# A graph kernel's attention and second spline: join and scans at the block's end, copies by the vector engine

## The reference

```python
# layer 0, attention with 4 heads: per edge a score, softmax over a node's edges, weighted sum
e = leaky_relu(a_src[:, src] + a_dst[:, dst] + fc_b[0], 0.2)
seg_max = segment_max(e.T, src)
e = exp(e - seg_max.T[:, src])
att = e / segment_sum(e.T, src).T[:, src]
agg = segment_sum(att * hp[:, dst, :], src)
...
# layer 3, second spline convolution: 125 kernels of 64 x 64, 8 of them weighted by a basis per edge
basis, idx = spline_basis(pseudo)
msg = einsum('es,eso->eo', basis, (x @ W)[col * K + idx])
out = segment_sum(msg, row) / max(deg, 1) + b
```

## Time and profile before

| what | us |
|---|---|
| median of 3 runs | 7320.52 (7303.47 to 7342.39) |
| the profiled execution | 7357.94 |
| its span | 7355.8 |
| PE busy | 4635.6 (63%) |
| DVE busy | 4183.0 (57%) |
| ACT busy | 1654.2 (22%) |
| POOL busy | 4443.2 (60%) |

### The profile page before, as it was taken

The page is one execution under the profiler, slowest core; times in us unless marked ns, Lnnn a source line. Parts: engine busy times, 40 slices in busy tenths (PEclk is TensorE's granted clock), DMA queues, the critical chain, the costliest instruction groups (busy, mean ns, idle before and its releaser), DMA issues. The chain is left out here.

```text
span 7355.8 us, 95916 instructions
## 1 busy us (share of the span) xinstructions
PE 4635.6 (63%) x31067; PEld 3408.4 (46%) x31067; DVE 4183.0 (57%) x9381; ACT 1654.2 (22%) x2811; POOL 4443.2 (60%) x4319
## 2 busy tenths in 40 slices
PE   5444442876638888888554667999992444544433
PEld 4444442655536666665443434555552333333322
DVE  7555553769946666666442316777773445444433
ACT  1111120117824444444231000000000222222211
POOL 2777776000057777777433256777764777777763
PEclk9999999569979999999776788999996777777766
DMA  4222221013332222224866581111111111111385
GB/s 73 78 71 78 71 78 26 21 36 151 160 76 54 52 53 53 54 52 49 37 30 180 195 270 39 38 37 37 37 34 23 19 18 18 19 19 18 17 14 14
DMA packets 388448, 441.47 MB, mean 60 GB/s; under 512 B 241139, under 2 KB 312320, under 8 KB 387981
## 3 DMA queue, kind: packets, MB, share of 16 engines
q0 software_dynamic: 137696, 130.26, 18.3%
q1 hardware_dynamic: 191113, 286.63, 12.4%
q10 hardware_dynamic: 59568, 23.69, 1.4%
HBM read 358.46 MB, written 82.34 MB: 60 GB/s over the span
## 5 line engine op out<-in xcount | busy, mean ns | idle before, releaser
L951 POOL DMA_INDIRECT at_far<-att_table,at_rec x1184 | 1227.7, 1037 | 886.0 <-DMA at_rec<-rec_r 400.9
L1524 POOL DMA_INDIRECT p_far<-table,p_rec x1184 | 1242.1, 1049 | 488.2 <-issue 359.9
L2162 PE MATMUL g_l_ps_sum<-g_l_row,g_l_of 128*128 128x392 f32 x3224 | 1062.9, 493 | 19.4 <-DVE g_l_of L2113 19.4
L534 POOL DMA_INDIRECT rec_r<-so_r_rec,so_r_place x806 | 835.0, 1036 | 245.5 <-issue 245.5
L2084 POOL DMA_INDIRECT g_l_got<-table,g_l_index x806 | 811.1, 1006 | 245.5 <-issue 228.4
L2162 PEld LDWEIGHTS g_l_ps_sum<-g_l_row,g_l_of 128*128 128x128 f32 x3224 | 613.2, 190 | 469.7 <-DVE g_l_of L2113 20.6
L1422 PE MATMUL p_ps_outer<-p_spread,p_basis 128*25 128x40 f32 (+1 forms) x4736 | 758.9, 341 | 77.9 <-DVE p_spread L1367 53.1
L1422 PEld LDWEIGHTS p_ps_outer<-p_spread,p_basis 128*25 128x25 f32 (+1 forms) x4736 | 636.0, 183 | 207.6 <-issue 94.5
L1422 PE MATMUL at_bank<-p_spread,p_basis 64*125 64x256 f32 x4736 | 629.3, 418 | 107.1 <-ACT p_outer L1477 107.1
L2096 DVE TENSOR_SCALAR g_l_row<-g_l_iota,edge_row 128x784 f32<-128x784 f32 x806 | 500.3, 693 | 222.2 <-PE g_l_ps_sum L2162 222.0
L489 PE MATMUL so_r_look<-so_r_table,so_r_lo_t 128*128 128x26 f32 x1612 | 425.0, 433 | 310.8 <-DVE so_r_table L433 310.8
(11 more groups left out here) (457 smaller groups left out, 6201.2 us busy)
## 6 DMA issues: line engine op xcount, KB each, us to landing
adjacent<-ad_by_chunk SPq DMA_DIRECT2D x74, 800.0 KB, 3.3
so_r_row<-pad_src SPq DMA_DIRECT2D x62, 832.0 KB, 6.2
g_l_counts<-adjacent SPq DMA_DIRECT2D x60, 800.0 KB, 6.9
g_l1d_counts<-adjacent SPq DMA_DIRECT2D x59, 800.0 KB, 7.1
so_r_low<-pad_lo_src SPq DMA_DIRECT2D x62, 416.0 KB, 4.7
at_far<-att_table,at_rec POOLq DMA_INDIRECT x1184
p_far<-table,p_rec POOLq DMA_INDIRECT x1184
rec_r<-so_r_rec,so_r_place POOLq DMA_INDIRECT x806, 2.1
```

The lines of the kernel that those rows point to most:

```text
L534: pool.indirect_dma_start(out=o.rec[:, :], out_offset=bass.IndirectOffsetOnAxis(ap=place[b][:, j:j + 1], axis=0), in_=rec[b][:, j, :], in_ ...
L951: pool.indirect_dma_start(out=far[b][:, t, :], out_offset=None, in_=g.att_table[:, :], in_offset=bass.IndirectOffsetOnAxis(ap=rec[b][:, t, ...
L1524: pool.indirect_dma_start(out=sl.far[b][:, t, :], out_offset=None, in_=table[:, :], in_offset=bass.IndirectOffsetOnAxis(ap=sl.rec[b][:, t, ...
L2162: last = nc.tensor.matmul(ps_sum[k][:], of4[b][:, j, :, :].rearrange("p k f -> p (k f)"), row1[b][:, j, k * COLS:(k + 1) * COLS], start=Fa ...
```

## The change

In DVE's order for block n: the differences of the maxima (`differences_of`) come right behind the basis, ahead of the lead spreads; the product with `keep` (`factors`) behind the lead spreads; the spline's scan of block n-1 stays behind at_spread; the copies of both results of block n-1 out of PSUM are made by DVE (`copy_rows`) between the spreads; and the join of block n stands at the end of block n itself. On ACT the exponentials of the differences come ahead of the sums' copy, and the stores of both results, with the load of the spline's marks, are issued in the block two later, behind the probabilities. PE's, SP's and POOL's programs stay as they are.

```diff
--- before.py
+++ after.py
@@ -1040,8 +1040,7 @@
                     ch.wait()
                     dve.sem_inc(scanned, 1)
 
-                def factors(n, b, turn):
-
+                def differences_of(n, b, turn):
 
                     dve.wait_ge(line_in[b], turn * 32 + 32)
 
@@ -1052,14 +1051,25 @@
                     ch.step(nc.vector.tensor_sub(fade[b][:, 1:V], upto[b][:, 0:V - 1], upto[b][:, 1:V]))
                     nc.vector.tensor_scalar(fade[b], fade[b], 0.0, None, ALU.min).then_inc(differences, 1)
 
+                def factors(n, b):
+
                     dve.wait_ge(exps, n * 2 + 2)
                     nc.vector.tensor_mul(fade[b], fade[b], keep[b][:]).then_inc(made, 1)
+
+                def copy_rows(n, b, turn):
+
+                    dve.wait_ge(rows_turned, n + 2)
+                    dve.wait_ge(rows_out[b], turn * 16 + 16)
+                    nc.vector.tensor_copy(rows[b][:], ps_rows).then_inc(rows_copied, 1)
+                    dve.wait_ge(sl.turned, n + 2)
+                    dve.wait_ge(sl.out, n * 16 + 16)
+                    nc.vector.tensor_copy(sl.rows[:], sl.ps_by_chunk).then_inc(sl.copied, 1)
 
                 ch.put(nc.vector.memset(run[1][:], 0.0))
                 ch.step(nc.vector.memset(upto[1][:], 0.0))
                 sl.begin_vector(dve, ch)
 
-                def one(n, b, turn, first=False, second=False):
+                def one(n, b, turn, first=False):
 
                     dve.wait_ge(turned, n + 2)
                     dve.wait_ge(near_in[b], turn * 16 + 16)
@@ -1073,20 +1083,24 @@
                     nc.vector.tensor_sub(shifted[:], leaky[:], top[b][:].unsqueeze(2).to_broadcast([P, C8, S])).then_inc(shifts, 1)
 
                     sl.points(dve, ch, n, b, turn, first=first)
+                    differences_of(n, b, turn)
                     sl.spread(dve, n, b, lead)
+                    factors(n, b)
 
                     dve.wait_ge(turned_back, n + 2)
                     dve.wait_ge(summed, n + 1)
                     nc.vector.tensor_mul(spread[:], ps_prob.unsqueeze(3).to_broadcast([P, TB, 4, C8]),
                                          o.mask[:].unsqueeze(1).unsqueeze(1).to_broadcast([P, TB, 4, C8])).then_inc(spreads, 1)
                     if not first:
-                        join(n - 1, 1 - b, second)
                         sl.scan(dve, ch, n - 1)
-                    factors(n, b, turn)
-                    sl.spread(dve, n, b, rest)
+                    sl.spread(dve, n, b, rest[:2])
+                    if not first:
+                        copy_rows(n - 1, 1 - b, turn + (b - 1))
+                    sl.spread(dve, n, b, rest[2:])
+                    join(n, b, first)
 
                 one(0, 0, 0, first=True)
-                one(1, 1, 0, second=True)
+                one(1, 1, 0)
                 with dve.Fori(1, o.pairs) as i:
                     ch.restart()
                     for b in two:
@@ -1094,8 +1108,8 @@
                 ch.restart()
                 if o.odd:
                     one(o.blocks - 1, 0, o.pairs)
-                join(o.blocks - 1, (o.blocks - 1) % 2, False)
                 sl.scan(dve, ch, o.blocks - 1)
+                copy_rows(o.blocks - 1, (o.blocks - 1) % 2, (o.blocks - 1) // 2)
 
             @block.scalar
             def _(act):
@@ -1108,15 +1122,15 @@
                     act.sem_inc(top_out[b], 16)
                     act.sem_inc(rows_out[b], 16)
 
-                def store_rows(n, b, turn):
-
-                    act.wait_ge(rows_turned, n + 2)
-                    act.wait_ge(rows_out[b], turn * 16 + 16)
-                    nc.scalar.copy(rows[b][:], ps_rows).then_inc(rows_copied, 1)
+                def store_rows(n, b):
+
                     act.wait_ge(rows_copied, n + 2)
                     act.dma_start(g.att_sums[bass.ds(n * V, V), :].rearrange("(q p) w -> p q w", p=P), rows[b][:]).then_inc(rows_out[b], 16)
-
-                def one(n, b, turn, first=False):
+                    act.wait_ge(sl.copied, n + 2)
+                    act.dma_start(sums64[bass.ds(n * V, V), :].rearrange("(q p) w -> p q w", p=P), sl.rows[:]).then_inc(sl.out, 16)
+                    sl.load_marks(act, n + 1)
+
+                def one(n, b, turn, first=False, second=False):
 
                     act.wait_ge(far_in[b], turn * (16 * TB) + 16 * TB)
                     act.wait_ge(turned, n + 1)
@@ -1126,6 +1140,12 @@
                     act.wait_ge(turned_back, n + 1)
                     nc.scalar.activation(prob[:], shifted[:].rearrange("p c s -> p (c s)"), ACT.Exp).then_inc(probs, 1)
                     act.dma_start(g.top[bass.ds(n * P, P), :], top[b][:]).then_inc(top_out[b], 16)
+                    if not first and not second:
+                        store_rows(n - 2, b)
+                    for k, exponent in enumerate((line[b], fade[b])):
+
+                        act.wait_ge(differences, n * 2 + (k + 1))
+                        nc.scalar.activation(exponent, exponent, ACT.Exp).then_inc(exps, 1)
 
                     act.wait_ge(summed, n + 2)
                     if not first:
@@ -1135,25 +1155,17 @@
                         half = slice(k * (TB // 2), (k + 1) * (TB // 2))
                         last = nc.scalar.copy(sums[:, :, half, :].rearrange("f h t c -> f t h c"), ps_sum[k])
                     last.then_inc(copied, 1)
-                    for k, exponent in enumerate((line[b], fade[b])):
-
-                        act.wait_ge(differences, n * 2 + (k + 1))
-                        nc.scalar.activation(exponent, exponent, ACT.Exp).then_inc(exps, 1)
-                    if not first:
-                        store_rows(n - 1, 1 - b, turn + (b - 1))
                     sl.copy_products(act, n)
-                    if not first:
-                        sl.store_rows(act, n - 1)
 
                 one(0, 0, 0, first=True)
-                one(1, 1, 0)
+                one(1, 1, 0, second=True)
                 with act.Fori(1, o.pairs) as i:
                     for b in two:
                         one(i * 2 + b, b, i)
                 if o.odd:
                     one(o.blocks - 1, 0, o.pairs)
-                store_rows(o.blocks - 1, (o.blocks - 1) % 2, (o.blocks - 1) // 2)
-                sl.store_rows(act, o.blocks - 1)
+                for n in (o.blocks - 2, o.blocks - 1):
+                    store_rows(n, n % 2)
                 sl.end_scalar(act)
                 for b in two:
                     act.wait_ge(rows_out[b], 16 * o.turns[b] + 16)
```

## The result

| | before | changed |
|---|---|---|
| median of 10 runs | 7328.75 (7303.47 to 7342.39) | 7374.19 (7358.73 to 7393.63) |
| ratio | | 1.0066 (1.0052 to 1.0081) |
| profiled execution, span | 7355.8 | 7384.7 |
| attention stage, first gather to last row store | 1823.1 | 1864.6 |

What follows compares the result with a forecast made beforehand. The other engines' chain was taken to set a quiet block at 44.4 us, GpSimd's gathers 1.6 us behind. Quiet part -19.8, tail +27.4, last block -3.5 gave +4.1, so 7325 us, range 7278 to 7372.

Steps and rivals of the forecast that it cites:

- C: Late blocks 30, 32, 34: line loads also land only with the drain; about +84, 7405; 16% for everything over 0.5% slower.
- GpSimd takes the place of the engines' chain: Attention stage: the engines' chain shrinks to about 39.5 us a block, GpSimd's gathers bound, the tail gives the rest back; 70%.
- What that rate is, is open ... so I take 43.5: GpSimd's gather rate in quiet blocks: 42.8 at best, 43.7 at worst, 43.5 us a block taken, giving -19.8 us.
- The first ten blocks were unhindered already: 0.: First ten blocks of the attention stage: GpSimd already waits for nobody there, so no gain, 0 us.
- The blocked tail, +27.4: Blocks 31, 33, 35: all work stands behind the late load of maxima, delaying the next gathers; +27.4 us, bounds 18 and 42.
- The last block, -3.5: Last block: no gathers behind it, chain shortened as in a quiet block, less end copies and stores; -3.5 us (-5 to -1).
- Copies by VectorE: Two more VectorE copies out of PSUM per block, 0.43 + 0.29 us, between the spreads; cost 0 to 0.3, 0.1 taken.
- Join at the end, late stores: Quiet blocks: join's 3.9 us move behind the last spread, ACT's stores two blocks later; loads and issues covered, no cost.
- Late blocks 30, 32, 34: Line load may be 2 to 6 us late there, covered by the gathers' backlog of over 10 us; cost 0.
- D: Small transfers pass the gathers' backlog, so the tail's 27.4 vanishes: -23.3, 7297; 3%, within the 70% of no change.
- the quiet part: Attention stage up to block 31: GpSimd's waits for p_spread vanish, part given back at 43.5 us a block; -19.8 us.

Runs made afterwards that it cites:

- the control: The kernel before, unchanged, run once more beside the last three experiments on a chip where PE is not held up: 7322.7 us.
- early against late differences: Early: changed kernel plus a VectorE wait between last difference and lead spreads, 7317.6. Late: changed kernel, differences and exponentials back in their old places, 7289.5.

## Why the prediction was wrong

The forecast was +4, 7325 (7278 to 7372); measured were +45 and 7374.2, 2 us above the range. The range stood on 7320.5, the median of three runs, where ten give 7328.75; on its own base +45 would have been 7366 and inside, near the upper end, but for a reason that no rival had. Slower by over half a per cent had 16%, all of it for the tail (C); no rival had a rate above 43.7 us a block.

- *GpSimd takes the place of the engines' chain.* Right: no wait for p_spread left, term waits for the gathers in 29 of 29 blocks, the chain of the other engines ends some 6 us before the gathers do (37.6 against 43.6 in the block shown).
- *"What that rate is, is open ... so I take 43.5", with 43.7 as the worst case.* This step failed. It measured 45.2. Early and later stretches of the kernel before bounded the rate for its own order of VectorE's work; the prediction said itself that the rate hangs on what VectorE runs in the same instant, and then took both bounds from stretches that don't have the new neighbours. The runs show what stands in their place: a gather that arrives within the last difference waits for all four lead spreads queued behind it, 3.0 to 3.3 us instead of 0.94, so 2.1 to 2.4 us a block. With one wait in between, or with the lead spreads in front, the rate is 43.35 and 43.5, the value forecast. That the value came out so exactly is in part luck, as it was chosen between bounds 0.9 us apart.
- *"The first ten blocks were unhindered already: 0."* Not so for the stage: at_score came every 44.05 us there in the kernel before. Without the long gather these blocks gain too: 29 us up to block 30 against the control on the same chip, where 19.8 were forecast.
- That a gather arrives there in every block fits the rows: a gather beside the scan L1048 takes 1.33 to 1.34 us, and the next comes 0.30 us behind its end, 0.18 or 0.19 us behind the start of the last difference in the blocks shown of seven versions. In 7 of the changed kernel's 28 blocks it starts 0.27 us into the first spread instead, and is held to the end of the fourth as well (3.03 us).
- *The blocked tail, +27.4.* Its mechanism is right: 26.8 us from the line load to the next gather, 31.1 to the next block. Its sum is rounded up by a microsecond: 24.3 + 2 - 16.8 is 9.5, not 9.7, and 28.4 + 2 - 23.1 is 7.3, not 8, so 26.3. Measured over the late blocks, +12.5 in the first pair of profiles and +33 if the second profile of before is taken instead, as two executions of one kernel on two chips differ by 20 us there (394.1, 373.7). The cleanest pair, early against late differences on one chip, gives 30.1, with one profile of each. The three waits for the load were forecast at about 30 us and are 34.1, 43.0 and 42.2, as the differences stand 11 us earlier in the block and the load lands when it did.
- *The last block, -3.5:* -6.3. *Copies by VectorE:* 0.42 and 0.28 us against 0.43 and 0.29, between the spreads, hidden; the gathers that start beside them take 0.94 or 0.95 us (16 of 16 in blocks 2 to 30), and the one of 1.42 us in the block shown starts within the spread ahead of them. *Join at the end, late stores:* waits for factors came to 2.7 us in the whole stage of the changed kernel. Right.
- *Late blocks 30, 32, 34.* Line loads late by 0.7 to 6.5 us, not more: rival C did not happen, nor D.
- Sum by its own steps with the rate measured: the quiet part +35 instead of -20 is 55 us, all of the miss and more; the tail took less than forecast by 15.
- By the inference in the Trainium skill (SBUF — State Buffer, "Who interferes with whom") GpSimd's rate would be unmoved by VectorE's two-operand work. The trace disagrees more strongly than before: 3.34 us beside four such spreads. The same section also says that an operation with two SBUF inputs contends with a GpSimd instruction that reads SBUF; these gathers read their indices from SBUF, so this sentence fits the rows, and the prediction did not weigh it.

## What to carry to other kernels

When the second limit is the issue of gathers by GpSimd, a shorter chain of the other engines is worth only the slack between them, here 1.6 us of 5, and its own rate must be asked for under the new order of VectorE's work. Look at the first gather that starts beside a reordered group of VectorE operations: an operation followed by a queue of others without a semaphore wait can shut it out for all of them, and here one wait, or another place, mended it. And an edit that puts a small DMA's result in front of a block's whole work cost nothing here while DMA was quiet and 10 us a block where it was backlogged, so place such a wait by the worst stretch.

## What was not expected of the hardware

- A gather's issue is held to the end of one VectorE operation behind the basis (1.46 to 1.49 us), and to the end of three to four spreads behind the small differences (3.0 to 3.9 us in five versions, every quiet block). A semaphore wait of VectorE, even one already all but fulfilled, lets it in (0.95 to 1.53 us). Neither the kind nor the width of the operation in front nor 0.7 us of shift changed it. Why the same four spreads behind eight basis operations don't do it is open.
- One program took 7323 us on one chip and 9495 on another, with PE waiting for single instructions. The changed kernel is 0.66% slower on the first chip and was 4% faster on that one, in a single execution.
- The backlog of the late blocks' gathers is in every profile but the four of that chip. There the late blocks take as long as the others (64 to 78 us), longer than the 56 us that I read for a block's gathers; that this is why was not tried.
